# One transformer block on one Trainium2 core: small on-chip tiles allocated behind the large ones

## The reference, cut to what matters

```python
x = x + xattn(layernorm(x), ctx, ctx, Wq, bq, Wk, bk, Wv, bv, Wo, bo)   # 16 heads of 16, 256 keys
x = x + attn(layernorm(x), w_qkv, b_qkv, w_out, b_out)                  # 16 heads, causal, 64 keys
x = x + ffn(layernorm(x), w_gate, w_up, w_down)                         # 256 -> 1024 -> 256

def _bitlinear(x, w):
    return einsum('bsi,oi->bso', _act_quant(x), _weight_quant(w))
```

## The kernel before, in words

| at 0 | at 32 |
|---|---|
| `id_sb`, `hm_sb`, `ca_sb`, `bv2_sb`, `wout_sb`, `w2oh`, `w2ol`, `bout_sb`, `x_all`, `xn`, `x_sb`, `c_sb`, `ch`, `cl`, `xnT`, `x1h`, `x1l`, `qb`, `k_sb`, `ones`, `hqT`, `y_sb` | `wq_sb` to `wo_sb` with all their high and low parts, `bv_sb`, `bo_sb`, `wqkv_sb`, `w2h`, `w2l`, `probs`, `hq_all`, `probsT`, `rm`, `r_sb`, `o_prod`, `oT`, `oh`, `ol`, `qT2`, `v_s1`, `v_s0`, `v2b`, `v2`, `id2_b`, `ca_b`, `nmax2`, `rsum2`, `rinv2`, `oT2`, `w_all`, `wb_all`, `xq`, `xqT` |

## Time and profile before

### The profile page before, as it was taken

The page is one execution under the profiler, slowest core; times in us unless marked ns, Lnnn a source line. Parts: engine busy times, 40 slices in busy tenths (PEclk is TensorE's granted clock), DMA queues, the critical chain, the costliest instruction groups (busy, mean ns, idle before and its releaser), DMA issues. The chain is left out here.

```text
span 879.9 us, 28583 instructions
## 1 busy us (share of the span) xinstructions
PE 848.6 (96%) x9750; PEld 713.0 (81%) x9750; DVE 756.9 (86%) x1583; ACT 694.0 (79%) x2045; POOL 483.4 (55%) x710
## 2 busy tenths in 40 slices
PE   7999999999999999999999997999999998999997
PEld 6889888988889888988988885888888875666664
DVE  6888888888888888888888887999999988999995
ACT  4778887777777777787777775888888877999996
POOL 3433334355554554334433326888787864777775
PEclk9999999999999999999999998999999999999999
DMA  4351111111011111111111000000000000000001
GB/s 136 111 179 51 48 42 30 50 44 48 30 42 48 31 43 45 42 48 30 42 48 36 13 2 1 3 1 1 0 1 0 1 2 1 31 31 30 34 33 36
DMA packets 31635, 31.84 MB, mean 36 GB/s; under 512 B 3280, under 2 KB 30800, under 8 KB 31568
## 3 DMA queue, kind: packets, MB, share of 16 engines
q1 hardware_dynamic: 30448, 30.47, 11.3%
q10 hardware_dynamic: 1120, 0.59, 0.2%
HBM read 26.86 MB, written 4.19 MB: 35 GB/s over the span
## 5 line engine op out<-in xcount | busy, mean ns | idle before, releaser
L520 ACT ACTIVATE probs<-psum,nmax 128x256 f32<-128x256 f32 x512 | 236.0, 488 | 56.9 <-DVE nmax L477 56.7
L551 POOL TENSOR_TENSOR rm<-rinv,hm_sb 128x256 f32<-128x256 f32 x64 | 39.8, 623 | 265.8 <-DVE rinv L449 265.8
L477 DVE TENSOR_REDUCE nmax<-psum 128x2 f32<-128x512 f32 x256 | 158.9, 683 | 11.5 <-PE psum L340 11.3
L353 PE MATMUL psum<-id_sb,probs 128*128 128x128 f32 x1024 | 125.9, 273 | 1.5 <-ACT probs L520 0.5
L353 PEld LDWEIGHTS psum<-id_sb,probs 128*128 128x128 f32 x1024 | 113.2, 141 | 5.5 <-ACT probs L520 5.3
L520 ACT ACTIVATION_READ_ACCUMULATOR probs<-psum,nmax 128x1 f32 x512 | 112.2, 219 | 0.0
L544 POOL TENSOR_TENSOR cl<-c_sb,ch 128x512 fp32r<-128x512 f32 x64 | 81.9, 1279 | 9.3 <-ACT ch L495 8.4
L340 PE MATMUL psum<-k_sb,qb 32*128 32x256 f32 x1024 | 74.3, 401 | 1.3 <-DVE qb L433 1.2
L528 POOL TENSOR_TENSOR rstd<-vare,minus_half 128x1 f32<-128x1 f32 x96 | 53.5, 558 | 30.5 <-DVE vare L410 26.5
L340 PEld LDWEIGHTS psum<-k_sb,qb 32*128 32x128 f32 x1024 | 46.7, 184 | 20.0 <-issue 17.9
L901 POOL TENSOR_TENSOR w_all<-c_sb,qm_sb 128x1024 f32<-128x1024 f32 x32 | 60.7, 1898 | 1.5 <-ACT c_sb L846 1.5
(11 more groups left out here) (176 smaller groups left out, 2503.6 us busy)
## 6 DMA issues: line engine op xcount, KB each, us to landing
c_sb<-in_ctx_t SPq DMA_DIRECT2D x64, 256.0 KB, 2.7
x_sb<-in_x SPq DMA_DIRECT2D x32, 128.0 KB, 2.4
out<-y_sb SPq DMA_DIRECT2D x32, 128.0 KB, 1.7
w_all<-in_w_gate SPq DMA_DIRECT2D x1, 1024.0 KB, 7.0
w_all<-in_w_up SPq DMA_DIRECT2D x1, 1024.0 KB, 6.8
w_all<-in_w_down SPq DMA_DIRECT2D x1, 1024.0 KB, 5.7
wqkv_sb<-in_w_qkv SPq DMA_DIRECT2D x1, 768.0 KB, 6.9
wk_sb<-in_wk ACTq DMA_DIRECT2D x1, 256.0 KB, 4.1
```

Of the source, the lines that this page charges most:

```text
L353: last = nc.tensor.transpose(sp[g][:, c:c + P], probs[:, 2 * g + u, kh * P:(kh + 1) * P], id_sb[:])
L477: nc.vector.tensor_reduce(nmax[:, 2 * g:2 * g + 2], sp[g].rearrange("p (u s) -> p u s", u=2), AX.X, ALU.max, negate=True).then_inc(max_don ...
L520: nc.scalar.activation(probs[:, j, :], sp[g][:, u * S:(u + 1) * S], ACT.Exp, bias=nmax[:, j:j + 1], accum_out=rsum[:, j:j + 1]).then_inc(e ...
L551: nc.gpsimd.tensor_tensor(rm[:].rearrange("p m (c e) -> p m c e", c=4), rinv[:].rearrange("p (c m) -> p m c", m=KT).unsqueeze(3) .to_broad ...
```

## The change

The calls that allocate 31 small tiles, of 4 to 48 bytes in a partition, move from between the large ones to the end of the list. Nothing else is touched: no instruction, wait, DMA or tile size. The order among the 31 stays, and so does the order among the 69 others. What follows for the starts, by the allocator's rule: of the 69, before the change 28 started at a multiple of 64 and 41 at 32 past one, and after it all 69 start at a multiple of 64; 63 of them hold 512 bytes or more, and of those 37 change. The first of the 31 then starts at byte 214464, and each of the 31 has the same remainder modulo 64 as before. The tiles `c_sb`, `x_sb`, `ch`, `cl` move by 448 bytes, from 192 past a multiple of 256 to a multiple of 256.

```diff
         id_sb = sb("id_sb", [P, P])
-        qm_sb = sb("qm_sb", [P, 2])
-        qm4_sb = sb("qm4_sb", [P, 4])
         hm_sb = sb("hm_sb", [P, 2 * E])
         ca_sb = sb("ca_sb", [P, L])
-        minus_half = sb("minus_half", [P, 1])
-        eps_col = sb("eps_col", [P, 1])
-        minus_one = sb("minus_one", [P, 1])
-        nmean = sb("nmean", [P, 1])
-        nmr = sb("nmr", [P, 1])
         wq_sb = sb("wq_sb", [P, KT, D])
...
-        stat = sb("stat", [P, 6])
-        mv = sb("mv", [P, 2])
-        vare = sb("vare", [P, 1])
-        rstd = sb("rstd", [P, 1])
         xn = sb("xn", [P, D])
...
-        nmax = sb("nmax", [P, PAIRS])
-        rsum = sb("rsum", [P, PAIRS])
-        rinv = sb("rinv", [P, PAIRS])
         probs = sb("probs", [P, PAIRS, S])
...
+        y_sb = [sb(f"y_sb{s}", [P, D]) for s in range(2)]
+
+
+        qm_sb = sb("qm_sb", [P, 2])
+        qm4_sb = sb("qm4_sb", [P, 4])
+        minus_half = sb("minus_half", [P, 1])
+        eps_col = sb("eps_col", [P, 1])
...
+        hscale = sb("hscale", [P, 1])
+        fd = [sb(f"fd{s}", [P, 1]) for s in range(2)]
```

More of the change, by code:

```diff
@@ L81, in block_kernel @@
         wo_sb = sb("wo_sb", [P, KT, D])
-        bq_sb = sb("bq_sb", [P, KT])
-        bk_sb = sb("bk_sb", [P, KT])
         bv_sb = sb("bv_sb", [P, D])
@@ L89, in block_kernel @@
                                 for w in (wqkv_sb, w2h, w2l)]
-        bqk_sb = sb("bqk_sb", [P, 2 * KT])
         bv2_sb = sb("bv2_sb", [P, D])
@@ L167, in block_kernel @@
         sc = w_all[:, 4:6, :].rearrange("p a (h l) -> p (a h) l", l=L)
+        ones = sb("ones", [P, P])
+        xq = sb("xq", [P, D])
+        xqT = sb("xqT", [P, KT, P], BF16)
+        hid = [probs[:, 4 * s:4 * s + 4, :].rearrange("p a b -> p (a b)") for s in range(2)]
+        hq = [hq_all[:, s, :] for s in range(2)]
+        hqT = sb("hqT", [P, IT, P], BF16)
+        y_sb = [sb(f"y_sb{s}", [P, D]) for s in range(2)]
[3 more added lines that the diff above has]
+        eps_col = sb("eps_col", [P, 1])
+        minus_one = sb("minus_one", [P, 1])
+        nmean = sb("nmean", [P, 1])
+        nmr = sb("nmr", [P, 1])
+        bq_sb = sb("bq_sb", [P, KT])
+        bk_sb = sb("bk_sb", [P, KT])
+        bqk_sb = sb("bqk_sb", [P, 2 * KT])
+        stat = sb("stat", [P, 6])
+        mv = sb("mv", [P, 2])
+        vare = sb("vare", [P, 1])
+        rstd = sb("rstd", [P, 1])
+        nmax = sb("nmax", [P, PAIRS])
+        rsum = sb("rsum", [P, PAIRS])
+        rinv = sb("rinv", [P, PAIRS])
         w_abs = sb("w_abs", [P, 12])
         w_sum = sb("w_sum", [P, 3])
-        ones = sb("ones", [P, P])
         w_mean = sb("w_mean", [P, 3])
@@ L176, in block_kernel @@
         fgu = [sb(f"fgu{s}", [P, 2]) for s in range(2)]
-        xq = sb("xq", [P, D])
-        xqT = sb("xqT", [P, KT, P], BF16)
-        hid = [probs[:, 4 * s:4 * s + 4, :].rearrange("p a b -> p (a b)") for s in range(2)]
         hmax = sb("hmax", [P, 1])
@@ L184, in block_kernel @@
         fd = [sb(f"fd{s}", [P, 1]) for s in range(2)]
-        hq = [hq_all[:, s, :] for s in range(2)]
-        hqT = sb("hqT", [P, IT, P], BF16)
-        y_sb = [sb(f"y_sb{s}", [P, D]) for s in range(2)]
         id_in = sem("id_in")
```

## The result

The changed kernel takes 885.12 us (884.55 to 887.3, 8 runs), the kernel before 882.69 us beside it (881.93 to 884.99, 8 runs). The ratio is 1.0028, with a 95% interval of 1.0017 to 1.0040: slower, by about 2.5 us. The forecast was no change, 882.6 us, in a range up to 884.6. The profiled execution took 884.75 us, its span is 882.9.

A forecast was written before the change was run, and what follows sets the result against it. The prediction took TensorE to bound stages 1 and 2, and VectorE and ScalarE to share the limit in stage 3. Every part came to 0, so it forecast no change, 882.6 us, in a range from 880.4 to 884.6.

The forecast's parts named there:

- What bounds the kernel: TensorE full in stages 1 and 2, VectorE and ScalarE sharing stage 3; 1 ns per stage 1 matmul is 6.1 us.
- Parts 1 and 2: TensorE's loaded and moving operands: a tile at 32 is no slower than one at 0; 0 us each.
- the 1.5 us kept for the range: Moving operand: the 1 ns difference seen, over 1,536 key and value matmuls, kept to either side.
- Rival (c): Key and value matmuls in stage 1: operands in the same position hinder each other; 6.1 us slower, 888.8 us; 5%.
- the signs named beforehand: If right: key and value matmuls 280 and 281 ns, loads 188, L977 1,283, TensorE about 508 us in the first stage.
- Parts 3 and 4: ScalarE, VectorE, GpSimd on large tiles, and stage 3's VectorE product: 0 us each, with ends of 2.0 us for stage 3.
- rival (a): Stage 3 product into probs pays for its address; 2.0 us come back, 880.6 us against the median; 6%.
- Part 5: The 31 small tiles keep remainder modulo 64 and order, getting other small tiles as neighbours; 0 us.
- Part 6: DMA: only waits at the start are exposed; 0 us, with ends of 0.5 us to either side.
- The saving that I had worked out from the Trainium skill: DMA transfers of c_sb and x_sb: 16% off each, some 0.4 us off the first waits, for 882.3.
- Rival (b): Handover to stage 2: the clock's fall to 1.2 GHz goes away; 2.5 us less, 880.1 us; 2%.
- The range: Whole kernel: 880.4 to 884.6 us, from a largest single bound of 2.0 us and 0.2 us of scatter.

The follow-up runs named there:

- e2: Changed kernel plus 32 bytes of padding in front of the projection weights and 32 behind them: 880.99 us, ratio 0.9992 to the kernel before.
- e3: Changed kernel plus 32 bytes of padding in front of xn, moving context, x and all behind, not the weights: 881.64 us, ratio 0.9995 to the kernel before.
- f4: Changed kernel plus 32 bytes of padding in front of wqkv_sb and 224 in front of x_all: 884.29 us, ratio 1.0018 to the kernel before.

## Why the prediction was wrong

**What bounds the kernel** was right, and with it the lever: TensorE is full in stages 1 and 2, and 1 ns per matmul is worth microseconds.

**Parts 1 and 2 failed**, "Worth: 0 us" for the loaded and for the streaming operand. The rows were read rightly: in the earlier trace rows one operand is at 32 and the other at 0 in both lines, in exchanged parts, and both take 188 and about 280 ns. But they show only that it doesn't matter *which* of the two is off. Every key and value matmul of the kernel before had its operands 32 bytes apart (modulo 256). The trace held no split-precision matmul at distance 0, and that is where the change put them all. So the rows couldn't price the change; the term was unknown, and the 1.5 us kept for the range was no bound. Measured: 3 ns from one start to the next in the value projection and 1 ns in the key projection, 2.9 us of work in stage 1, of which 2.5 us arrived there. The split-precision matmuls of stage 2 had no term at all; they add 1.2 us of work.

**Rival (c) named the mechanism**, its place, its sign and the point from which it decides (1.2 ns). I gave it 5%, because of the earlier trace rows: both operands at 32 took 379 ns as did the pair that differs. That evidence failed twice. By the allocator's rule `oT` starts 64 bytes past `wo_sb` modulo 256, so that pair was not in the same position either. And it is another kind of matmul: L389 is in full precision and starts every 216 ns, the split-precision ones every 117; L389 kept 650 ns for its four in every kernel of this study, at all eight distances. The price was too high: the key and value groups grew by (35 + 12) / 11 / 2 = 2.1 ns a step, 3.0 us, where I had 4 ns and 6.1 us. The "277 to 281 ns in one group" behind it was also misread: the earlier trace rows has 277 to 282 for the value group.

Of the signs named beforehand, the loads (192 for 188) and the value matmuls (283 for 280) told it; TensorE's 508 us in the first stage did not, since a full engine stays full when its work grows.

**Parts 3 and 4** held: L976 is at 1,283 ns, L981 at 1,220, and rival (a) with its 2.0 us is out. **Part 5** held: e2 and e3 leave the small tiles at the end and show no loss. **Part 6** held in its number, and bears on the page: after the change `c_sb` and `x_sb` start at a multiple of 256, and their landings in the changed kernel's list of DMA issues are

```profile
c_sb<-in_ctx_t SPq DMA_DIRECT2D x64, 256.0 KB, 2.7
x_sb<-in_x SPq DMA_DIRECT2D x32, 128.0 KB, 2.4
```

the same as in the earlier trace rows. The saving that I had worked out from the Trainium skill ("DMA: Bandwidth & Descriptors", section "How a descriptor splits into AXI transactions") does not appear here on the side that writes on-chip memory, neither in the medians nor in the first waits for `x_sb`, 2.7 us where they were 2.4, nor in the time that the packets of this queue took, 11.4% of the 16 engines' span where it was 11.3%. No run here shows the side that reads.

**Rival (b)**, the clock: in the profiled execution the stretch at 1.2 GHz was shorter, 3.4 us for 6.9, and the total was slower nonetheless. Its length differs between runs, so this neither bears (b) out nor refutes it. **The range** ended at 884.6 because it was built from parts 2, 4 and 6 and left (c) out, the one rival whose place and sign came true.

## What to carry to other kernels

Where TensorE is the bound and runs short split-precision matmuls back to back, the place of the two operand tiles against each other modulo 256 bytes was worth 0.6% of the time here, from 879.5 to 885.1 us in the medians, for at most 224 bytes of padding. Scan it with a padding tile, and measure before rounding tiles to a common boundary. The best distance was not the same for every projection. When a change puts two things into the same position, rows in which only one of them varies don't price it, however well they agree; look for a row with the pair, of the same kind of instruction, and if there is none, widen the range.

## What the runs showed of the hardware that was not expected

- In the value projection the time from one split-precision matmul's start to the next (256 columns, full clock) depends on where its operands lie against each other: from (1263 / 11 =) 114.8 ns at a distance of 192 to 120.0 ns at 0. The numbers came back after a shift of 256 bytes (f4). At 0 the median is 120 in each place of the group, while at 160 the places' medians lie between 116 and 125 ns.
- The same kernels' full-precision output projection (L389, 216 ns a start) kept its time at all eight distances, and the transposes of `probs` (L353, 109 ns a start) in every kernel.
- No effect of a start at 0 or 32 modulo 64 on ScalarE, VectorE or GpSimd beyond 1% of a group's mean, and none of 192 against 0 modulo 256 on the landing of the loop's DMAs, could be seen.
- Why the cost has this shape, with a sign and with 160 as bad as 0 for one kind of matmul, is open, and so is why the query projection answers otherwise than the key projection at the same distance. Distances finer than 32 bytes were not tried.
